# The start and the end of two state-space mixers: first chunk projected from centred values, half of its convolution on VectorE, softplus in halves, last output projection block by block

## The reference

```
h  = layernorm(x);  hn = rmsnorm(h) * w
xc, z = split(hn @ inproj.T)             # 256 -> 2 x 512
u  = silu(causal_conv(xc, 4 taps) + b)
dt, B, C = split(u @ xproj.T)            # 512 -> 64 (layer 1: 16) + 16 + 16
dt = softplus(dt @ dtw.T + dtb)          # -> 512
per token t:  state = exp(dt*A)*state + (dt*u)*B[t];  y = sum_n(state*C[t]) + u*D
out = (y * silu(z)) @ outproj.T  (+ h)   # 512 -> 256
layer 0: out = rmsnorm(out + h) * normf, in both directions, summed
```

## Time and profile before

| | us |
|---|---|
| median of 3 runs (lowest to highest) | 2744.15 (2742.71 to 2744.16) |
| the profiled execution's own time | 2750.91 |
| its span in the trace | 2748.8 |
| TensorE busy | 2400.8 (87%) |
| VectorE busy | 1871.0 (68%) |
| GpSimd busy | 1555.8 (57%) |
| ScalarE busy | 1318.9 (48%) |

### The profile page before, as it was taken

How to read it: one execution, slowest core, us unless ns; L and a number is a source line. 1 busy time by engine, 2 the same in 40 slices (tenths; PEclk the granted TensorE clock), 3 DMA queues, 4 the chain that set the end, 5 groups by cost and what they waited for, 6 DMA issues and landing times. The chain is left out here.

```text
span 2748.8 us, 27150 instructions
## 1 busy us (share of the span) xinstructions
PE 2400.8 (87%) x8488; PEld 1097.0 (40%) x8488; DVE 1871.0 (68%) x2555; ACT 1318.9 (48%) x2085; POOL 1555.8 (57%) x1370
## 2 busy tenths in 40 slices
PE   7889899898997769889999679999798989788878
PEld 3333333333332224343333368888432333233322
DVE  1999999999999964367775430110369999994334
ACT  4556565665656434435666322222156566443433
POOL 2999999999999951140000122222159999993110
PEclk9999999999999989999999889999799999999989
DMA  4030311303123000042220145554330230300000
GB/s 163 37 123 1 146 65 65 130 9 123 34 90 111 13 3 21 29 128 46 48 48 2 36 169 191 183 179 153 111 124 34 90 124 1 123 0 21 1 9 31
DMA packets 66260, 207.15 MB, mean 75 GB/s; under 512 B 15531, under 2 KB 35510, under 8 KB 47558
## 3 DMA queue, kind: packets, MB, share of 16 engines
q1 hardware_dynamic: 55988, 167.05, 17.9%
q10 hardware_dynamic: 5714, 26.32, 2.9%
q0 software_dynamic: 4416, 12.06, 1.4%
HBM read 187.89 MB, written 17.30 MB: 75 GB/s over the span
## 5 line engine op out<-in xcount | busy, mean ns | idle before, releaser
L896 POOL TENSOR_TENSOR s_dbu<-s_dx,s_bc 128x512 f32<-128x512 f32 x768 | 966.4, 1284 | 26.4 <-DVE s_psum L564 24.6
L480 PE MATMUL s_psum<-s_hc,ident 128*128 128x512 f32 x1536 | 821.1, 626 | 162.4 <-DVE s_hc L584 143.1
L759 ACT ACTIVATE s_psum<-s_dt,s_a_neg 128x512 f32<-128x512 f32 x768 | 521.7, 688 | 574.8 <-DVE s_hc L584 573.8
L480 PEld LDWEIGHTS s_psum<-s_hc,ident 128*128 128x128 f32 x1536 | 259.4, 191 | 663.6 <-DVE s_hc L584 428.9
L584 DVE TENSOR_TENSOR s_hc<-s_psum,s_bc 128x512 f32<-128x512 f32 x624 | 422.8, 678 | 0.4 <-issue 0.4
L564 DVE TENSOR_TENSOR_SCAN s_psum<-s_psum,s_state,s_dbu 128x512 f32<-128x512 f32 x312 | 396.6, 1285 | 11.2 <-POOL s_dbu L896 6.6
L564 DVE TENSOR_TENSOR_SCAN s_psum<-s_psum,s_dbu 128x512 f32<-128x512 f32 x312 | 381.5, 1223 | 15.0 <-POOL s_dbu L896 12.6
L2015 ACT ACTIVATE s_probs<-s_banks 128x512 f32<-128x512 f32 (+3 forms) x384 | 169.5, 495 | 117.2 <-PE s_banks L1724 85.9
L2449 ACT ACTIVATE s_hidden<-s_banks,s_w 128x256 f32<-128x256 f32 x184 | 77.1, 470 | 253.9 <-PE s_banks L2241 253.9
L907 POOL TENSOR_TENSOR s_hc<-s_hs,s_bc 128x512 f32<-128x512 f32 x144 | 182.9, 1270 | 14.7 <-DVE s_hs L564 14.7
L432 PE MATMUL s_psum<-s_pad,s_taps 128*128 128x512 f32 x384 | 191.2, 592 | 0.0
(11 more groups left out here) (325 smaller groups left out, 3284.7 us busy)
## 6 DMA issues: line engine op xcount, KB each, us to landing
s_bc<-fwd_rows SPq DMA_DIRECT2D x64, 1024.0 KB, 4.7
s_bc<-m_rows SPq DMA_DIRECT2D x32, 1024.0 KB, 4.7
s_w<-in_moe_w SPq DMA_DIRECT2D x23, 1028.0 KB, 4.8
s_w<-in_moe_w ACTq DMA_DIRECT2D x23, 1024.0 KB, 5.3
qk_parts<-s_parts SPq DMA_DIRECT2D x48, 128.0 KB, 1.9
s_stack_q<-qk_parts SPq DMA_DIRECT2D x96, 64.0 KB, 2.4
s_stack_k<-qk_parts SPq DMA_DIRECT2D x48, 128.0 KB, 4.4
x<-in_xT SPq DMA_DIRECT2D x4, 512.0 KB, 6.2
```

The costliest lines, as they stand in the source:

```text
L480: pe.matmul(psum[:, SCANS + block_no % 2, :], consts["ident"][:], hc[:, unit % PRODUCTS, :], start=(n == 0), stop=(n == NS - 1)).then_inc( ...
L759: act.activation(psum[:, unit % SCANS, :], dt[:, g % 2, i // NS, :], ACT.Exp, scale=a_neg[CHUNKS[g][0]][:, i:i + 1]).then_inc(decay_ready, 1)
L896: pool.tensor_tensor(dbu[:, unit % TERMS, :], dx[:, g % 2, i // NS, :], bc[:, 2 * n, :], ALU.mult)\
```

## The change

Only `mixers` changes (and the host's `mamba_arrays`, which adds the taps as columns, `_fold`). In words:

1. SP's order: x chunk 0, half of the input weights, x chunk 1, the small columns and the fold columns, the first half of the taps, `w_x`, `w_dt`, x chunks 2 and 3, then the rest.
2. The norm's weight is multiplied into the first half of the input weights by VectorE, ahead of its first `center`. Chunk 0 is projected from the centred `res`, without the root; VectorE multiplies by the root as it moves the result to `pad` (`keep_first_x`).
3. Means of chunks 1 to 3 and variances of chunks 0 and 1 are made from sums of the two blocks that GpSimd adds first: one matmul each in place of two. Variances 2 and 3 move into the loop, at i 2, 3 and 8, 9.
4. Blocks 0 and 1 are convolved by TensorE, blocks 2 and 3 by VectorE with four operations each (`fold`).
5. Softplus of chunk 0 goes in halves of two blocks. max(v, 0) of blocks 0 and 1 is made by VectorE, and has its own place (`dt[:, 1]`), so `begin_pad(1)` no longer waits for the additions. Blocks 2 and 3 are finished in the loop: exp and ln at i 2 on ScalarE, additions and products on GpSimd at i 18, 20, 22, 24.
6. `scale_xn` of chunks 2, 3 moves from i 4, 8 to i 14, 20. `scale_res` of chunks 0, 1 moves to VectorE before the loop, that of chunks 2, 3 from i 12, 18 to i 35, 40 (GpSimd).
7. At the end the matmuls with `res` go to i 58, 59, those with gated blocks 0 and 1 to i 62, 63, block 2 and 3 behind the loop. VectorE gates the last block, scales straight out of PSUM and adds to x; ScalarE's copies are gone.

```diff
-        for kind, count in (("x", EB), ("conv", EB), ("rows", 1), ("dt", EB)):
+        for kind, count in (("conv", KD), ("rows", 1), ("dt", EB)):
...
+            load_x(0)
             sp.dma_start(w_in[:, :, 0:EI], dram[f"{first}_in"][:, :, 0:EI]).then_inc(in_x_loaded, 16)
-            sp.dma_start(taps[:], dram[f"{first}_taps"]).then_inc(taps_loaded, 16)
+            load_x(1)
...
+            sp.dma_start(state[:, 0:TAPS * EB], dram[f"{first}_fold"]).then_inc(small_loaded, 16)
+            sp.dma_start(taps[:, 0:KD * TAPS, :], dram[f"{first}_taps"][:, 0:KD * TAPS, :]).then_inc(taps_first_loaded, 16)
...
+            def first_in_x(m):
+                if m == 0:
+                    pe.wait_ge(x_scaled, KD)
+                    pe.wait_ge(ln_centered, 1)
                 for k in range(KD):
+                    mm = pe.matmul(first_bank(m), w_in[:, k, m * P:(m + 1) * P], res[:, k, at(0)],
                                    start=(k == 0), stop=(k == KD - 1))
+                mm.then_inc(first_x, 1)
...
+            def last_out(m, k):
+                w = tile["out", NC - 1, m]
+                pe.wait_ge(last_gated, 1) if k == EB - 1 else pe.wait_ge(y_ready, EB * (NC - 1) + k + 1)
+                mm = pe.matmul(bank(w), w_out[:, k, m * P:(m + 1) * P], dx[:, (NC - 1) % 2, k, :], start=False, stop=(k == EB - 1))
...
             mean(0)
+            first_in_x(0)
             mean(1)
+            first_in_x(1)
             variance(0)
+            first_in_x(2)
+            first_in_x(3)
+            variance(1)
+            for m in range(KD):
+                first_conv(m)
+            for n, k in enumerate((0, 2, 3, 1)):
+                first_rows(k, n)
             mean(2)
+            steps_of(0, 0)
+            steps_of(0, 1)
             mean(3)
+            steps_of(0, 2)
+            steps_of(0, 3)
...
+                    if g == 0 and i in (2, 3):
+                        late_variance(2, i - 2)
+                    if g == 0 and i in (8, 9):
+                        late_variance(3, i - 8)
...
+                    if g == NC - 1 and i in (58, 59):
+                        last_res(i - 58)
+                    if g == NC - 1 and i in (62, 63):
+                        for m in range(KD):
+                            last_out(m, i - 62)
+            for k in (2, 3):
+                for m in range(KD):
+                    last_out(m, k)
...
+            def keep_first_x(m):
+                dve.wait_ge(first_x, m + 1)
+                dve.wait_ge(rms_rstd_ready, 1)
+                dve.tensor_tensor(pad[:, m, TAPS - 1:TAPS - 1 + CH], first_bank(m), rms_rstd[0], ALU.mult)\
+                   .then_inc(first_kept, 1)
...
+                    dve.scalar_tensor_tensor(out=total_u, in0=pad[:, m, j:j + CH], scalar=tap, in1=total_u,
+                                             op0=ALU.mult, op1=ALU.add).then_inc(folded, 1)
...
+            for k in range(KD):
+                scale_first_in(k)
             center(0)
             center(1)
-            scale_xn(0)
+            for m in range(KD + 1):
+                keep_first_x(m)
+            fold(2, 0)
+            keep_first_x(3)
+            fold(3, 0)
+            for j in range(1, TAPS):
+                for m in (2, 3):
+                    fold(m, j)
+            for c in range(2):
+                scale_xn(c)
+                scale_first_res(c)
             center(2)
-            scale_xn(1)
             center(3)
-            dve.wait_ge(soft_ready, 1)
-            for e in range(EB):
-                dve.tensor_tensor(dt[:, 0, e, :], dt[:, 0, e, :], relu[:, e, :], ALU.add).then_inc(dt_ready, 1)
+            for m in range(KD):
+                first_relu(m)
+            for e in range(KD):
+                w = tile["dt", 0, e]
+                dve.wait_ge(half_ready, 1)
+                dve.wait_ge(work_free[w % 2], w // 2 + 1)
+                dve.tensor_tensor(dt[:, 0, e, :], dt[:, 0, e, :], relu_of(0, e), ALU.add).then_inc(dt_ready, 1)
...
+            last_gate()
             if post is not None:
                 for m in range(KD):
-                    scale_y(NC - 1, m)
+                    last_scale(m)
+            for m in range(KD):
+                last_add(m)
...
             store_rows(0)
-            square_x(3)
-            for m in range(EB):
-                store_steps(0, m)
-            soft_exp(0)
-            soft_log(0)
-            rms_of(2)
-            ln_of(2)
+            first_abs(0)
+            first_abs(1)
+            first_soft(0)
+            for m in (2, 3):
+                first_abs(m)
+                first_relu(m)
+            square_x(2)
...
+                    if g == 0 and i in (18, 22):
+                        add_relu(0, 2 + (i - 18) // 4)
+                    if g == 0 and i in (20, 24):
+                        times_u(0, 2 + (i - 20) // 4)
+                    if g == 0 and i in (35, 40):
+                        scale_res(2 if i == 35 else 3)
```

More of the change, by code:

```diff
@@ L316, in mixers @@
                 place("dt", g + 1, EB)
-            if g and post is not None:
+            if g and g < NC and post is not None:
                 place("var", g - 1, 1)
@@ L398, in mean @@
             def mean(c):
-                if source is not None:
-                    pe.wait_ge(source_loaded[c], 16)
-                for k in range(KD):
-                    mm = pe.matmul(stat(c, 0), consts["ones"][:], x[:, k, at(c)], start=(k == 0), stop=(k == KD - 1))
+                if c:
+                    pe.wait_ge(ln_paired, c)
+                    if c >= 2:
+                        pe.wait_ge(ln_centered, c - 1)
+                    mm = pe.matmul(stat(c, 0), consts["ones"][:], hc[:, c % 2, :], start=True, stop=True)
+                else:
+                    if source is not None:
+                        pe.wait_ge(source_loaded[0], 16)
+                    for k in range(KD):
+                        mm = pe.matmul(stat(0, 0), consts["ones"][:], x[:, k, at(0)], start=(k == 0), stop=(k == KD - 1))
@@ new lines, in first_conv, with first_rows @@
+            def first_conv(m):
+                w = tile["conv", 0, m]
+                pe.wait_ge(taps_first_loaded, 16)
+                pe.wait_ge(front, 1)
+                pe.wait_ge(first_kept, m + 1)
+                for j in range(TAPS):
+                    mm = pe.matmul(bank(w), taps[:, m * TAPS + j, :], pad[:, m, j:j + CH], start=(j == 0), stop=(j == TAPS - 1))
+                mm.then_inc(work_ready[w % 2], 1)
+            def first_rows(k, n):
+                w = tile["rows", 0, 0]
+                if n == 0:
+                    pe.wait_ge(x_loaded, 16)
+                if k < KD:
+                    source = tile["conv", 0, k]
+                    pe.wait_ge(work_free[source % 2], source // 2 + 1)
+                else:
+                    pe.wait_ge(fold_silu, k - KD + 1)
+                mm = pe.matmul(bank(w)[0:XD], w_x[:, k, :], u[:, 0, k, :], start=(n == 0), stop=(n == EB - 1))
+                if n == EB - 1:
+                    mm.then_inc(work_ready[w % 2], 1)
@@ new lines, in last_gate, with last_scale @@
+            def last_gate():
+                e, part = EB - 1, dx[:, (NC - 1) % 2, EB - 1, :]
+                dve.wait_ge(gate_ready, NC)
+                dve.wait_ge(y_read, NC * EB)
+                dve.tensor_tensor(part, part, gate[:, e, :], ALU.mult).then_inc(last_gated, 1)
+            def last_scale(m):
+                w = tile["out", NC - 1, m]
+                dve.wait_ge(last_rstd, 1)
+                dve.scalar_tensor_tensor(out=y[(NC - 1) % 2][:, m, :], in0=bank(w), scalar=post[:, m:m + 1],
+                                         in1=u[:, (NC - 1) % 2, KD, :], op0=ALU.mult, op1=ALU.mult).then_inc(last_scaled, 1)
@@ new lines, in last_add @@
+            def last_add(m):
+                w = tile["out", NC - 1, m]
+                if post is not None:
+                    dve.wait_ge(last_scaled, m + 1)
+                    more = y[(NC - 1) % 2][:, m, :]
+                else:
+                    dve.wait_ge(work_ready[w % 2], w // 2 + 1)
+                    more = bank(w)
+                dve.tensor_tensor(tokens(x, m, NC - 1), tokens(x, m, NC - 1), more, ALU.add).then_inc(x_added, 1)
+            for k in range(KD):
+                scale_first_in(k)
@@ L764, in _ @@
             square_x(1)
-            rms_of(0)
-            ln_of(0)
-            square_x(2)
-            act.wait_ge(small_loaded, 32 * len(runs))
+            for c in range(2):
+                rms_of(c)
+                ln_of(c)
+            act.wait_ge(small_loaded, 32 * len(runs) + 16)
             for r in range(len(runs)):
```

204 lines of the change are left out of this document (135 added, 69 removed).

## The result

The changed kernel takes 2705.49 us (median of 4 runs, 2703.16 to 2707.36), the kernel before 2743.43 (4 runs of the same session). The ratio is 0.987, with a 95% interval from 0.9854 to 0.9886: 37.9 us faster. The prediction said 2683.0, in a range of 2671 to 2700. The sign was right, the size was not: 23 of the 61 us are missing, and the time lies outside the range.

What follows compares the result with a forecast made beforehand. It read a loop near balance (stage 0: VectorE busy 925.55, GpSimd 915.38 of 1028.8 us) with the loss mostly at its two ends. 24.0 + 19.3 + 10.4 + 8.4 - 1 = 61.1 off 2744.15 gave 2683, range 2671 to 2700.

Steps and rivals of the forecast that it cites:

- The ends: Ends of stages 0 and 3, after the last scan: 10.4 and 8.4 us gained.
- The half convolution: Start of each stage: 16 convolution records on TensorE instead of 32, folds hidden beside them, 6.9 us gained.
- Rival B: Both starts: VectorE becomes the bound, folds at 1.85 us, centres some 8 us later each; 2699 us, chance 0.12.
- The starts: Stage start to first scan: 24.0 us gained in stage 0, 19.3 in stage 3.
- rival A: Starts and ends: TensorE stays at 1.2 GHz, costing 20 us over four stretches; 2703 us, chance 0.12.
- The price of a fold: VectorE's eight folds in each start: 0.72 us each because GpSimd is nearly idle, not 1.85.
- sign of being wrong: Named failures: folds averaging over 1 us, the second clock level holding in the convolution, chunk 0 over 122 us.
- Chunk 0's loop: Work moved into chunk 0's loop costs between -1 and +5 us per stage, taken as 0.5, two stages 1.
- GpSimd's part of the same step: Chunk 0's loop: GpSimd's four added operations, 4.9 us between i 18 and 24, set against its waits of 2.9 + 2.1.
- Rival C: Chunk 0's loop stalls on late GpSimd additions or bank waits behind queued work; 2750 us, chance 0.03.
- The base: Whole kernel: profiled execution 2750.91 us, median 6.8 lower at 2744.15, from which the gain was subtracted.

Runs made afterwards that it cites:

- e3: The kernel before with only the change's new end (part 7): 2725.20 us against 2744.29, ratio 0.9936.
- e11: The kernel before, unchanged, profiled once more to see how much its stretches vary: one run, 2739.41 us.
- e8: The changed kernel with all four blocks of chunk 0's convolution on TensorE and no folds on VectorE: 2720.00 us, ratio to before 0.9914.
- e9: The changed kernel with chunk 2's variance made before the loop and chunk 3's root at i 17 instead of 14: 2701.19 us, ratio to before 0.9845.
- e7: The changed kernel with e1 and e4 together, GpSimd's residual scalings at i 18 and 24, and chunk 3's root at i 17: 2694.02 us.
- e4: The changed kernel with softplus, additions and products of chunk 0's blocks 2 and 3 finished before the loop, the latter two by VectorE: 2700.30 us.
- e5: e4 with GpSimd's scalings of the residual at i 18 and 24 instead of 35 and 40: 2704.11 us, ratio to before 0.9858.
- e12: e9 with GpSimd's residual scalings back at i 18 and 24, its four additions and products staying in the loop: 2701.40 us.
- e2: The changed kernel with additions and products of blocks 2 and 3 on VectorE at i 16 and 22 instead of GpSimd: 2710.71 us.
- e1: The changed kernel with chunk 2's variance made by TensorE before the loop: 2699.61 us, ratio to before 0.9838.
- e6: The changed kernel without three of the four taps of chunk 1's convolution (output then differs): 2707.64 us, ratio to before 0.9865.

## Why the prediction was right in sign and wrong in size

- **The ends: right.** 10.5 and 8.4 against 10.4 and 8.4, alone too (e3, 19.1). Skip and gate lie behind the last scan, VectorE adds last. That the figures agree to 0.1 is in part luck: the kernel before's second trace (e11) has ends 1.3 and 1.7 shorter.
- **The half convolution: right.** Sixteen records in 7.03, the folds done first (30.94 against 32.05), the last six of them in 4.48; taken back in e8 it costs 16 records, 6.9, as in the sum (first scans 4.7 and 7.6 later). Rival B falls.
- **The starts: right in mechanism, 0.6 to 2.8 short.** Up to the rows each step came within 1.4 us: projection 13.61 (13.4), end of the convolution 32.05 (30.7), rows' copy 35.52 (34.3). All four records of block 0 had the slow price (3.75), where I gave it to two, 0.9 more. Then the four records of the step sizes of blocks 2 and 3 took 3.78 behind an idle 1.98, where the four of blocks 0 and 1 took 1.98; the granted clock of 41.3 to 45.0 was 0.50, that is 1.2 GHz. That is 1.8 us of rival A. ScalarE's decay was last, as forecast.
- **The price of a fold: right where GpSimd is idle.** 0.74 each for five of the eight. GpSimd scaled weights from 24.44 to 27.95, beside the first three, and those show the price beside a busy GpSimd: of the two that only multiply the first took 0.49 and the second 0.90, and the first of the six that also add, at 26.46, took 1.17 (1.17 in stage 3 too). Not 1.85, but half as much again as 0.74. The eight average 0.78, under the 1 us that would have been a sign of being wrong.
- **Chunk 0's loop: the step that failed.** "Cost between -1 and +5 for each stage; I take 0.5 ... because its idle time is about its new work." It cost 8.1 and 8.0, above my upper bound, so 15 of the missing 23 us, and 127 is over the 122 that I had named as a sign of being wrong. Of this, 3.0 in each stage is ScalarE's in-order wait for a late variance (e9), which I had not priced at all. The rest, 5.3 and 4.1 (e7 against e9), came back when the second half of the softplus, GpSimd's four operations and its scalings all went to other places. Of it 1.8 lie in units 0 to 12, before any of GpSimd's moved work. There TensorE is late, 9.0 behind the first scan; without the softplus in ScalarE's loop it came in 7.2 (e4) and 6.3 behind (e7). I had not priced that either.
- **GpSimd's part of the same step.** What is left, 3.6 and 2.4, lies where GpSimd's pieces stand. For these I set GpSimd's idle time of 5.0 against 4.9 of new work. But those waits were eleven pieces of at most 0.7: each is a moment in which GpSimd was as far ahead as it can be, three units. In the changed kernel its waits were 12.1, and still none stood where the new work did. My reading, which no run shows alone, is that the new operations use up the lead, and that the loop is balanced, so nothing wins it back. Moving the scalings moved the loss (e5, e12); handing the four operations to VectorE inside the loop did not end it (e2), doing them before the loop did (e7).
- **Rival C had the mechanism and the wrong price.** "If a bank handed over between TensorE, ScalarE and VectorE waits for work queued behind it, the loop stalls": that is the 5.35 us at 64.88. I gave it 0.03 because I asked only when it would eat all 61 us. It should have been a term of the sum, with a price for each wait.
- **The base: 4.6 us too long.** The profiled execution of before lay 6.8 over the median, and I took that off at the end as if it lay anywhere. The traces with the code of before (three for the starts, two for the ends) say that most of it lay where the change works: its starts are 2.5 and 0.6 over their means, its ends 0.7 and 0.8.

| us | forecast | profiled pair | means of the traces |
|---|---|---|---|
| start, stage 0 | 24.0 | 21.2 | 66.65 - 46.44 = 20.2 |
| start, stage 3 | 19.3 | 18.7 | 58.27 - 40.52 = 17.8 |
| ends | 18.8 | 18.9 | 9.8 + 7.6 = 17.4 |
| chunk 0, two stages | -1 | -16.1 | -16.1 |
| sum | 61.1 | 42.7 | 39.3 |

(Starts of before: 69.12, e3 64.52, e11 66.32, and 58.91, 57.94, 57.96. Of the change: its own, e1, e2, e6, e9, e12: 47.92, 45.37, 45.84, 46.01, 47.77, 45.72, and 40.26, 41.05, 40.32, 40.37, 40.27, 40.83. Ends from the traces of before and e11.) The sum of 39.3 stands beside the measured 37.9. The 21.8 between 61.1 and 39.3 are 15.1 of the loop, 4.6 of the base and 2.1 of the starts' own steps.

What stays open: e7 took from the loop both GpSimd's four operations and ScalarE's second half of the softplus, so how the 5 us divide between them is shown only as far as the units show it: 1.8 are not GpSimd's, and of the rest TensorE's lateness may have a part, since it still holds GpSimd up by 1.3 at 76.85 in e9. No run has GpSimd's operations in the loop with the softplus before it. Between e1 and e9 only the second root moves. It takes 2.1 off chunk 0 of stage 3 (126.1 to 124.0) and nothing off that of stage 0 (124.0 in both); why stage 0 doesn't gain is open too.

## What to carry to other kernels

Work moved into a balanced loop is not free because the receiving engine's waits sum to as much: look at where the waits stand and at the longest single one, and if the new piece is longer, charge it in full (here 4.9 us of work and what came with it cost 4.4 and 5.6 behind unit 12, e12 against e7). The same loop index is another time on each engine, so where the change adds a wait between two engines that run ahead and behind, compare the two absolute times in the trace (here ScalarE's i 8 at 59.5 against TensorE's i 3 at 63.8) and charge what the in-order queue holds up. When reading sums of waits, see which of them stand before the stretch begins: 2.4 of the 6.5 did here. If the profiled execution is above the median, look first whether the excess lies in the stretches that the change shortens.

## What the runs showed of the hardware that I had not expected

**Who pays where GpSimd and VectorE meet.** Two groups, GpSimd's copy of 128x12 before (mean 371 ns) and after:

```profile
L856 POOL COPY s_pad<-s_pad 128x12 f32<-128x12 f32 x6 | 2.2, 371 | 31.0 <-DVE s_dt L618 31.0
```
```profile
L1042 POOL COPY s_pad<-s_pad 128x12 f32<-128x12 f32 x6 | 7.5, 1253 | 8.4 <-PE s_psum L460 8.4
```

The two long ones, one in each stage, took 3.35 and 3.36 us beside VectorE's scalings with two inputs in SBUF, which kept their 1.21. The one of stage 0 began at 32.19, while such a scaling ran, and ended at 35.54, just behind the last of them (35.48). When GpSimd ran full terms of 128x512, VectorE paid too: in the timeline of the change the product by u ahead of GpSimd's first term (43.29) took 0.69, and the one beside it 1.64.

```profile
42.52 0.69 DVE L773 TENSOR_TENSOR s_dx<-s_dt,s_u 128x512 f32<-128x512 f32 x1
...
43.84 1.64 DVE L773 TENSOR_TENSOR s_dx<-s_dt,s_u 128x512 f32<-128x512 f32 x1
```

The addition between them (43.13 to 43.81) kept its 0.68, though the term began at 43.29, so not every such operation pays.

The Trainium skill, GPSIMD Engine Reference, section 8, Key points, says that GpSimd shares its SBUF interfaces with VectorE and contends with VectorE's instructions that have two SBUF inputs. The trace agrees, and shows the cost on either side.

**A start that varies.** The first scan of stage 0 of the same code came at 64.52, 66.32 and 69.12. The mean of chunk 0 and 1 took 5.35, 5.86 and 6.74 for eight records, and the weights landed so that GpSimd's first scaling began at 15.56, 15.86 and 17.60. That is 4.6 us between executions of one start. The changed start varies too, mostly ahead of the copy of the rows: from the copy of the rows to the first scan of stage 0 it took 12.40 in the changed kernel, e2, e6 and e8 alike (12.41 in e9), but the four records of block 0's projection took 3.75 in the changed kernel and 1.96 in e1, and with them the copy came at 35.52 and at 33.53. The profile's clock row says 1.00 for 13.5 to 17.0 in both, so it doesn't show why.
